# A chunked linear-attention recurrence on 32x32 tiles: delta and state in two halves, each with its own PSUM bank and copy

## The chip, the core and the metric

The kernel runs on one core of a Trainium2 chip. What counts is the device time of one execution in microseconds (us). PE is TensorE (PEld its weight loads), DVE VectorE, ACT ScalarE, POOL GpSimd, SP the SyncE queue that issues the DMAs.

## The reference

One transformer block in Macaron form over 8192 tokens of width 512. Only the middle part is touched: attention of the gated-delta kind with 16 heads of width 32, whose state is carried from token to token.

```python
def _step(Sm, inputs):
    q_t, k_t, v_t, beta_t = inputs
    Sk = jnp.einsum('bhde,bhe->bhd', Sm, k_t)
    delta = v_t - Sk
    Sm = Sm + beta_t[..., None] * jnp.einsum('bhd,bhe->bhde', delta, k_t)
    o_t = jnp.einsum('bhde,bhe->bhd', Sm, q_t)
    return (Sm, o_t)
...
return outputs @ wo + bo
...
x = x + 0.5 * _L0_ffn_ref(_layernorm(x, axis=-1), ...)
x = x + _L0_attn_ref(_layernorm(x, axis=-1), ...)
x = x + 0.5 * _L0_ffn_ref(_layernorm(x, axis=-1), ...)
```

The attention part ends in a feed-forward network of width 2048, for which the kernel splits fp32 factors into two fp32r parts, high and low, and multiplies three times.

## The kernel before, in words

There are three stages. The first (to about 960 us) makes heads, keys and the inner products of the keys and writes them to HBM. The second (about 960 to 1726 us) is the recurrence, and the change lies in it alone. The third (to the end) is the feed-forward network.

The recurrence goes over 256 chunks of 32 tokens. The 16 heads lie as 4 partition groups by 4 column groups, so each product of a chunk is 16 matmuls of 32x32 (function `tiles`); the trace has two passes for each, so 16 matmuls are an x32 of weight loads and of matmuls. A chunk needs six such products, and I call them by their functions: `values` and `keys` (from `ringA`, what DMAs bring), `delta` (`sT` times `nR`, onto `values`), `state` (`de` times `ringB`), and the outputs `out_state` and `out_delta`. Between them ACT copies PSUM to SBUF: `de` after `delta`, `sT` after `state`, `nR` after `keys`. So the chain that carries the state is: delta on PE, copy de, state on PE, copy sT, delta of the next chunk. PE fills the time of a copy with the products of other chunks: `values` and `keys` of a chunk to come, the outputs of a chunk gone by.

PE's program is a real loop (`Fori`) of 64 turns, each one block of 128 tokens, four chunks, and one output product: 12 matmuls of 128x512 with `wo` (`out_product`), for the block before. Since a turn's waits count upward, they wait on registers and stand on an instruction that adds to the register. The other engines' programs are written out, in order of the chunk c, with blk and at from divmod(c, 4). ACT's `high(q)` takes the outputs of a pair of chunks from PSUM as fp32r, DVE's `low(q)` makes the remainder; only when both are there for the pairs of a block may the output product of the block begin (PE waits for `v_olo`). DVE's `add_out` adds the product to `zb`, which ACT made with `normalize` and POOL added a bias to with `add_bo`.

Beside this DVE and POOL solve the triangular systems of chunks 32 and more ahead: `solver(c, 0)` and `solver(c, 1)`, two slots in each chunk with a table of steps that is spread evenly by size. DVE has three of the four column groups (L1474, L1478) and transposes in and out (L1452, L1462), POOL the fourth. In every second block from block 6 to 36 ACT and DVE also split a piece of a weight (DVE's L1517).

SP brings `ringA` and `ringB`, four slots each, in the order of its program; a load of a slot waits until PE is done with it.

## Time and profile before

| | |
|---|---|
| median of 3 runs | 3310.53 us (3310.06 to 3311.02) |
| the profiled execution, its span | 3309.8 us |
| PE busy | 3179.2 us, 96% |
| DVE busy | 1841.6 us, 56% |
| ACT busy | 1308.4 us, 40% |
| POOL busy | 1205.1 us, 36% |
| recurrence, first to last row of its loop | 971.3 to about 1726 us |

The span is the time from the first to the last instruction; here it is within 1 us of the runs' median. PE's busy share says little in the recurrence: a 32x32 matmul takes some 190 ns from start to end but one starts every few ns, so the engine reads as busy through every short wait. What counts there is the time from one start to the next.

### The profile page before, as it was taken

To read this page: it belongs to the slowest core of one execution; us is meant where nothing else is said; L and a number is where in the kernel's file an instruction comes from. 1 tells how busy PE (TensorE), PEld (TensorE's weight loads), DVE (VectorE), ACT (ScalarE), POOL (GpSimd) and SP (SyncE) were. 2 spreads that over 40 slices of the span, in tenths; PEclk is the share of its full clock that TensorE was granted. 3 is DMA by queue.
4 is the path that set the end of the run, shared out by engine and by line. 5 is a ranking of instruction groups with operands and counts; after the bars stand their busy time and mean duration, and the time that the engine had idled before them with its cause. 6 is when DMAs were issued, how large, how long until landed. Compare 5 with 4: busy or idle time off the path is not lost.

```text
span 3309.8 us, 150288 instructions
## 1 busy us (share of the span) xinstructions
PE 3179.2 (96%) x68438; PEld 2594.1 (78%) x68438; DVE 1841.6 (56%) x2965; ACT 1308.4 (40%) x2654; POOL 1205.1 (36%) x1211
## 2 busy tenths in 40 slices
PE   5999999999958999999999999999999999999998
PEld 4777777777747888898888778887777888777886
DVE  6787878778648899888323333233333323333324
ACT  5444445444313333333343333333333433333333
POOL 1435564655526776666211222211222212122211
PEclk8999999999969999999999999999999999999999
DMA  3445555455465677666661110101110110111010
GB/s 111 144 148 167 141 162 154 145 152 162 139 201 181 220 227 228 215 197 207 200 184 35 39 39 13 39 26 39 39 39 17 36 39 26 39 39 38 14 39 26
DMA packets 388865, 356.00 MB, mean 108 GB/s; under 512 B 58256, under 2 KB 321680, under 8 KB 385680
## 3 DMA queue, kind: packets, MB, share of 16 engines
q1 hardware_dynamic: 386400, 351.86, 34.2%
q8 instruction: 154, 2.52, 0.3%
q10 hardware_dynamic: 2224, 0.90, 0.2%
q14 instruction: 87, 0.71, 0.1%
HBM read 184.65 MB, written 153.09 MB: 102 GB/s over the span
## 4 chain that ended last, share of the span: by engine, by line
PE 65%; DMA 2%; SPq 0%; DVE 0%; issue 0%; ACT 0%; DVEq 0%; ACTq 0%
PE bank L237 14%; PE bank L235 14%; PE bank L236 14%; PE bank L1238 13%; PE bank L1283 5%; PE bank L1698 2%; PE bank L1689 2%; DMA ringB<-heads_scratch 1%; PE bank L1681 1%; PE bank L1672 1%; DMA Z<-z_scratch 0%; DVE g L2010 0%; PE bank L1745 0%; SPq L1147 0%; ACT relu L1867 0%
## 5 line engine op out<-in xcount | busy, mean ns | idle before, releaser
L1939 DVE TENSOR_TENSOR glo<-gl,gh 128x512 fp32r<-128x512 f32 x256 | 196.0, 766 | 823.5 <-ACT gh L1817 821.8
L1813 ACT ACTIVATE gl<-bank,b1m 128x512 f32<-128x512 f32 x256 | 176.0, 687 | 736.4 <-PE bank L237 730.9
L235 PE MATMUL bank<-h,w_hi 128*128 128x512 f32 x1024 | 421.1, 411 | 0.1
L235 PE MATMUL bank<-w_hi,gh 128*128 128x512 f32 x1024 | 402.7, 393 | 0.9 <-DVE glo L1939 0.9
L237 PE MATMUL bank<-h,w_lo 128*128 128x512 f32 x1024 | 401.3, 392 | 0.0
L237 PE MATMUL bank<-w_hi,glo 128*128 128x512 f32 x1024 | 400.5, 391 | 0.0
L236 PE MATMUL bank<-h,w_hi 128*128 128x512 f32 x1024 | 399.4, 390 | 0.0
L236 PE MATMUL bank<-w_lo,gh 128*128 128x512 f32 x1024 | 399.2, 390 | 0.0
L236 PEld LDWEIGHTS bank<-h,w_hi 128*128 128x128 f32 x1024 | 193.4, 189 | 49.2 <-issue 10.7
L235 PEld LDWEIGHTS bank<-h,w_hi 128*128 128x128 f32 x1024 | 192.5, 188 | 48.7 <-issue 10.8
L1238 PE MATMUL bank<-ringA 32*32 32x32 f32 x16512 | 221.9, 196 | 5.3 <-issue 4.3
L2076 POOL TENSOR_TENSOR ss<-ss,cst 128x4 f32<-128x4 f32 x15 | 15.3, 1017 | 578.7 <-DVE ss L1922 578.7
L236 PEld LDWEIGHTS bank<-w_lo,gh 128*128 128x128 f32 x1024 | 193.5, 189 | 40.2
L237 PEld LDWEIGHTS bank<-h,w_lo 128*128 128x128 f32 x1024 | 192.3, 188 | 40.8
L235 PEld LDWEIGHTS bank<-w_hi,gh 128*128 128x128 f32 x1024 | 192.5, 188 | 40.1 <-DVE glo L1939 1.3
L237 PEld LDWEIGHTS bank<-w_hi,glo 128*128 128x128 f32 x1024 | 192.3, 188 | 39.8
L967 POOL TENSOR_TENSOR nrm<-nrm,cst 128x16 f32<-128x16 f32 x64 | 185.4, 2897 | 101.3 <-DVE nrm L761 100.6
L1238 PEld LDWEIGHTS bank<-ringA 32*32 32x32 f32 x16512 | 192.1, 105 | 9.8 <-issue 4.6
L1474 DVE TENSOR_TENSOR tmp<-sysf 128x90 f32<-128x90 f32 (+14 forms) x210 | 189.5, 902 | 5.0
L2085 POOL TENSOR_TENSOR Z<-Z,H 128x512 f32<-128x512 f32 x64 | 92.5, 1445 | 273.0 <-DMA H<-x_scratch 273.0
L1478 DVE TENSOR_TENSOR sysf<-sysf,tmp 128x90 f32<-128x90 f32 (+14 forms) x210 | 183.7, 875 | 4.8
L1564 POOL TENSOR_TENSOR zb<-zb,bo 128x512 f32<-128x512 f32 x64 | 93.8, 1465 | 245.7 <-ACT zb L1400 132.0
(200 smaller groups left out, 7086.1 us busy)
## 6 DMA issues: line engine op xcount, KB each, us to landing
ringB<-heads_scratch SPq DMA_DIRECT2D x257, 192.0 KB, 3.3
ringA<-heads_scratch SPq DMA_DIRECT2D x260, 128.0 KB, 2.8
X<-in_L_attn_x SPq DMA_DIRECT2D x16, 1024.0 KB, 10.1
x_scratch<-X SPq DMA_DIRECT2D x16, 1024.0 KB, 4.5
heads_scratch<-vb SPq DMA_DIRECT2D x16, 1024.0 KB, 5.2
heads_scratch<-qk SPq DMA_DIRECT2D x16, 1024.0 KB, 6.6
heads_scratch<-kb SPq DMA_DIRECT2D x16, 1024.0 KB, 5.2
heads_scratch<-kbuf SPq DMA_DIRECT2D x16, 1024.0 KB, 7.2
```

What stands on the lines that cost most here:

```text
L235: e.matmul(o, lhs[0], rhs[0], start=first, stop=False)
L236: e.matmul(o, lhs[0], rhs[1], start=False, stop=False)
L237: return e.matmul(o, lhs[1], rhs[0], start=False, stop=last)
L967: e.tensor_tensor(nrm[:, u], nrm[:, u], pos_half.broadcast_to([P, TC]), ALU.pow).then_inc(o_pow, 1)
L1238: m = e.matmul(out[r, n, :], lhsT[r, n, :], rhs[r, n, :], start=first and n == 0, stop=True, skip_group_check=True)
L1283: m = e.matmul(bank[B_WO][:, :], oh[x][:, f, :], wo[y][:, f, :], start=k == 0, stop=k == 11)
L1474: e.tensor_tensor(tt, N[:, :, j + 1:CH, j:j + 1].broadcast_to([P, 3, rows, j]), N[:, :, j:j + 1, 0:j].broadcast_to([P, 3, rows, j]), ALU.m ...
L1478: e.tensor_tensor(N[:, :, j + 1:CH, 0:j], N[:, :, j + 1:CH, 0:j], tt, ALU.add).then_inc(v_sol, 1)
L1564: e.tensor_tensor(zb[i][:, :], zb[i][:, :], bo[:, :], ALU.add).then_inc(o_yb, 1)
L1813: e.activation(gl[k][:, :], bank[1 - k][:, :], ACT.Gelu_apprx_tanh, bias=b1m[:, m:m + 1]).then_inc(a_gl, 1)
L1939: e.tensor_tensor(gh[k][1][:, :], gl[k][:, :], gh[k][0][:, :], ALU.subtract).then_inc(v_gl, 1)
L2085: e.tensor_tensor(z[:, b, :], z[:, b, :], H[:, b, :], ALU.add).then_inc(o_zx, 1)
```

## The change

`delta` and `state` are each made in two halves of the column groups (0 and 1: FRONT, 2 and 3: BACK), each with its own PSUM bank, its own increment and its own ACT copy of 64 columns in place of one of 128. `values` and `out_delta` are halved with them; `keys` and `out_state` stay whole. The outputs of a chunk are now made within the chunk (before they came one to three chunks later). The output product moves from the end of the loop's turn to its middle, behind chunk 1. PE's waits for ACT and the DMAs are on constants, with one semaphore for each of the four chunks, and PE takes the count back with increments by -2, -16 and -32 on its own matmuls. Only the waits for DVE (`v_olo`, `v_z`) still go by a register. On ACT and DVE the steps of a block stand at other chunks: `high` and `low` at 0 and 2 (before 0 and 1), `normalize` at 1, `add_out` and the piece of a weight at 3, `add_bo` at 2. SP's loads are reordered. The core of the diff:

```diff
-        B_WO, B_R, B_DELTA, B_STATE, B_OUT = 0, (1, 3), (4, 5), 6, (7, 2)
+        B_WO, B_R, B_DELTA, B_STATE, B_OUT = 0, 1, (4, 5), (6, 3), (7, 2)
...
-        a_wohi, a_delta, a_state, a_y2, a_ohi = sems("a_wohi a_delta a_state a_y2 a_ohi")
+        a_wohi, a_y2, a_ohi = sems("a_wohi a_y2 a_ohi")
+        a_delta, a_state = sems("a_delta0 a_delta1 a_delta2 a_delta3"), sems("a_state0 a_state1 a_state2 a_state3")
...
-                if c >= 4 and c % 4 < 2:
-
-                    e.wait_ge(p_delta, max(1, c - 4))
-                elif c >= 4:
-                    e.wait_ge(p_R, c - 3)
+                if c >= 4:
+                    e.wait_ge(p_delta, 2 * (c - 4) + 1)
...
-                    e.wait_ge(p_o, c - 2)
-                e.dma_start(ringB[:, c % 4, :, :], heads_d[c if c < CHUNKS else c - 4, :, Q2:B2 + 1, :]).then_inc(d_B[c % 4], 16)
+                    e.wait_ge(p_o, c - 3)
+                elif c == 3:
+                    e.wait_ge(p_delta, 1)
+                e.dma_start(ringB[:, c % 4, :, :], heads_d[c, :, Q2:B2 + 1, :]).then_inc(d_B[c % 4], 16)
...
             for blk in range(NBLK + 1):
                 c = 4 * blk
-                if c + 6 < CHUNKS + 4:
-                    load_a(c + 6)
-                if blk and c + 3 < CHUNKS:
-                    load_b(c + 3)
-                if c + 7 < CHUNKS + 4:
-                    load_a(c + 7)
                 if c + 4 <= CHUNKS:
+                    load_a(c + 4)
+                if c + 4 < CHUNKS:
                     load_b(c + 4)
+                if blk >= 2:
+                    store_z(blk - 2)
+                if c + 5 < CHUNKS:
+                    load_a(c + 5)
+                    load_b(c + 5)
...
-                if blk >= 2:
-                    store_z(blk - 2)
+                if c + 6 < CHUNKS:
+                    load_a(c + 6)
+                    load_b(c + 6)
                 if 1 <= blk and blk + 1 < NBLK:
                     load_x1(blk + 1)
...
+                if c + 7 < CHUNKS:
+                    load_a(c + 7)
+                    load_b(c + 7)
...
             def tiles(out, lhsT, rhs, first):
 
-                for n in range(GROUPS):
+                made = []
+                for n in range(out.shape[1]):
                     for h in range(4):
                         r = slice(32 * h, 32 * h + 32)
...
+
+            def place(h):
+
+                return split(bank[B_DELTA[h]][:, 0:P // 2])
...
+            def values(j, h):
+
+                return tiles(place(h), split(ringA[:, j, RX, :])[:, own(h), :], split(ringA[:, j, RV, :])[:, own(h), :],
+                             True)
...
+            def delta(j, h):
+
+                made = tiles(place(h), nR[j % 2][:, own(h), :], sT[j][:, own(h), :], False)
+                made[-1].then_inc(p_delta, 1)
+                return made
...
+            def state(j, h):
+
+                tiles(split(bank[B_STATE[h]][:, 0:P // 2]), split(ringB[:, j, RB, :])[:, own(h), :],
+                      de[j % 2][:, own(h), :], False)[-1].then_inc(p_state, 1)
+
+            def out_delta(j, h):
...
+            def chunk(j):
+
+                after, before = (j + 1) % 4, (j + 3) % 4
+                e.wait_ge(a_state[j], 1)
+                made = delta(j, FRONT)
+                made[0].then_inc(d_A[j], -32)
+                made[1].then_inc(a_delta[before], -2)
+                made[2].then_inc(d_B[before], -16)
+                e.wait_ge(d_A[after], 32)
+                keys(after)
+                e.wait_ge(a_state[j], 2)
+                delta(j, BACK)
+                e.wait_ge(d_B[j], 16)
+
+            def outs_back(j):
+
+                made = out_delta(j, BACK)
+                made[0].then_inc(a_state[j], -2)
+                made[-1].then_inc(p_o, 1)
+
+            def rest(j):
+
+                after = (j + 1) % 4
+                out_state(j)
+                e.wait_ge(a_delta[j], 1)
+                state(j, FRONT)
+                values(after, FRONT)
+                out_delta(j, FRONT)
+                e.wait_ge(a_delta[j], 2)
+                state(j, BACK)
+                values(after, BACK)
...
-                ahead(j)
-
-            e.wait_ge(d_A[2], 32)
-            e.wait_ge(d_A[3], 32)
-            e.wait_ge(d_B[0], 16)
+            e.wait_ge(o_s0, 1)
+            for h in (FRONT, BACK):
+                e.matmul(bank[B_STATE[h]][:, 0:P], heads(sT[0][:, :, :]), heads(sT[0][:, :, :]), start=True, stop=True)
+            e.wait_ge(a_delta[3], 2)
             e.wait_ge(d_B[3], 16)
...
-            with e.register("now") as now, e.register("out") as out, e.register("slot_a") as slot_a, \
-                    e.register("next_a") as next_a, e.register("slot_b") as slot_b, e.register("next_b") as next_b:
...
+            keys(0)
+            values(0, FRONT)
+            values(0, BACK)
...
                              hint_back_edge=True, head_slot={mybir.EngineType.PE: 0}):
-                    for j in range(4):
-                        e.wait_ge(a_state, now)
-                        if j == 3:
-                            e.wait_ge(v_olo, out)
-                        e.reg_add(now, now, 1)
...
-                        e.wait_ge(a_delta, now)
...
-                            out_state(3)
-                            out_delta(3)
-                        elif j == 1:
...
-                        else:
-                            e.wait_ge(v_z, out)
-                            e.reg_add(out, out, 4)
-                            out_product(range(12))
-                            e.reg_add(slot_b, slot_b, 16)
...
+
+                    chunk(0)
+                    e.wait_ge(v_olo, out)
+                    e.reg_add(out, out, 4)
+                    rest(0)
+                    outs_back(0)
+
+                    chunk(1)
+                    rest(1)
+                    e.wait_ge(v_olo, out)
+                    e.reg_add(out, out, 4)
+                    e.wait_ge(v_z, done)
+                    e.reg_add(done, done, 8)
+                    outs_back(1)
+                    out_product(range(12))
+
+                    for j in (2, 3):
+                        chunk(j)
+                        rest(j)
+                        outs_back(j)
+
...
             def delta(c):
-                e.wait_ge(p_delta, c + 1)
-                e.activation(heads(de[c % 2][:, :, :]), bank[B_DELTA[(c // 2) % 2]][:, c % 2 * P:(c % 2 + 1) * P],
-                             ACT.Copy).then_inc(a_delta, 2)
+                for h in range(2):
+                    e.wait_ge(p_delta, 2 * c + h + 1)
+                    e.activation(heads(de[c % 2][:, 2 * h:2 * h + 2, :]), bank[B_DELTA[h]][:, 0:P // 2],
+                                 ACT.Copy).then_inc(a_delta[c % 4], 1)
...
-                e.wait_ge(p_o, 2 * q + 3)
+                e.wait_ge(p_o, 2 * q + 2)
...
                     keys(c + 1)
                 state(c)
-                if at < 2 and blk:
-                    high(2 * blk - 2 + at)
+                if at == 0 and blk:
+                    high(2 * blk - 1)
+                elif at == 2:
+                    high(2 * blk)
                 if c == 0:
                     for k in range(NF):
                         split_wo(k)
-                if at == 0 and blk:
+                if at == 1 and blk:
                     normalize(blk - 1)
                 i = piece2(blk)
...
             for c in range(CHUNKS):
                 blk, at = divmod(c, 4)
-                if at == 0 and blk >= 2:
-                    add_out(blk - 2)
+                if at == 3 and blk:
+                    add_out(blk - 1)
                 solver(c, 0)
-                if at < 2 and blk:
-                    low(2 * blk - 2 + at)
+                if at == 0 and blk:
+                    low(2 * blk - 1)
+                elif at == 2:
+                    low(2 * blk)
                 i = piece2(blk)
-                if at == 2 and i is not None:
+                if at == 3 and i is not None:
                     e.wait_ge(a_w1hi, i + 1)
...
-            e.memset(sT[3][:, :, :], 0.0).then_inc(o_s0, 1)
-            e.memset(de[1][:, :, :], 0.0).then_inc(o_s0, 1)
             e.memset(sT[0][:, :, :], 0.0).then_inc(o_s0, 1)
+            e.memset(de[1][:, :, :], 0.0).then_inc(a_delta[3], 2)
+            e.memset(ringB[:, 3, :, :], 0.0).then_inc(d_B[3], 16)
             for c in range(CHUNKS):
                 blk, at = divmod(c, 4)
-                if at == 1 and blk:
+                if at == 2 and blk:
                     add_bo(blk - 1)
```

PE, the part of the loop's turn with the output product, before (`de,ringB` is `state`, L1283 the product):

```order
L1238 MATMUL bank<-ringA 32x32 x16
L1334 REGISTER_ALU [waits d_B3,a_delta]
L1238 MATMUL bank<-de,ringB 32x32 x16
L1349 REGISTER_ALU [waits v_z]
L1283 MATMUL bank<-wo_hi,oT_hi 128x512
L1283 MATMUL bank<-wo_lo,oT_hi 128x512
```

and of the change, behind `state` and `values` of chunk 1 (L1315 is the product):

```order
L1233 MATMUL bank<-de,ringB 32x32 [waits a_delta1]
L1233 MATMUL bank<-de,ringB 32x32 x7
L1233 MATMUL bank<-ringA 32x32 x8
L1346 REGISTER_ALU [waits v_olo]
L1348 REGISTER_ALU [waits v_z]
L1233 MATMUL bank<-ringB,de 32x32 x8
L1315 MATMUL bank<-wo_hi,oT_hi 128x512
```

The wait for DVE's `low` stands right ahead of the product now; before, it stood at chunk 3's `delta`, and the instruction in front of the product waits for `v_z` alone.

DVE, from one `low` to the second next (`oT_lo`), in blocks whose solver steps lie alike, before:

```order
L1491 TENSOR_TENSOR oT_lo<-bank,oT_hi 128x4x64 [waits a_ohi]
L1478 TENSOR_TENSOR sysf<-sysf,tmp 128x3x21x10 [waits v_sol]
L1474 TENSOR_TENSOR tmp<-sysf 128x3x220 [waits v_sol]
L1517 TENSOR_TENSOR w_lo<-Z,w_hi 128x512 [waits a_w1hi]
L1478 TENSOR_TENSOR sysf<-sysf,tmp 128x3x20x11 [waits v_sol]
L1474 TENSOR_TENSOR tmp<-sysf 128x3x228 [waits v_sol]
L1478 TENSOR_TENSOR sysf<-sysf,tmp 128x3x19x12 [waits v_sol]
L1497 TENSOR_TENSOR zb<-bank,zb 128x512 [waits o_yb,p_wo]
L1474 TENSOR_TENSOR tmp<-sysf 128x3x234 [waits v_sol]
L1491 TENSOR_TENSOR oT_lo<-bank,oT_hi 128x4x64 [waits a_ohi]
```

and of the change, from the `low` at chunk 2 to the `low` at chunk 0 of the next block:

```order
L1491 TENSOR_TENSOR oT_lo<-bank,oT_hi 128x4x64 [waits a_ohi]
L1478 TENSOR_TENSOR sysf<-sysf,tmp 128x3x20x11 [waits v_sol]
L1497 TENSOR_TENSOR zb<-bank,zb 128x512 [waits o_yb,p_wo]
L1474 TENSOR_TENSOR tmp<-sysf 128x3x228 [waits v_sol]
L1519 TENSOR_TENSOR w_lo<-Z,w_hi 128x512 [waits a_w1hi]
L1478 TENSOR_TENSOR sysf<-sysf,tmp 128x3x19x12 [waits v_sol]
L1474 TENSOR_TENSOR tmp<-sysf 128x3x234 [waits v_sol]
L1491 TENSOR_TENSOR oT_lo<-bank,oT_hi 128x4x64 [waits a_ohi]
```

Before, the two `low` of a block stand one chunk apart and the rest of the block's work lies behind the second; now they stand two chunks apart, and between the second and the first of the next block lie four solver slots, `add_out` and the piece of a weight.

## Rows read from the trace of the kernel before

**Rows 1.** Stages: busy time by engine (instructions), PEclk, DMA share, GB/s.

```profile
1016.70:1056.00 39.30, 35.66 (x2491) 31.88 (x2478) 38.15 (x43) 13.09 (x48) 37.11 (x35) 0.96 0.71 225
...
1077.60:1592.80 515.20, 509.20 (x35885) 458.97 (x35884) 460.21 (x550) 192.75 (x705) 352.63 (x409) 1.00 0.70 215
1592.80:1609.20 16.40, 13.14 (x781) 11.74 (x780) 8.47 (x7) 4.63 (x17) 1.28 (x1) 0.79 0.76 209
1609.20:1721.00 111.80, 110.75 (x7820) 99.85 (x7822) 17.06 (x35) 42.89 (x158) 13.65 (x11) 1.00 0.67 199
```

**Rows 2.** Timeline, PE, one turn: start, duration, instruction.

```profile
1425.59 0.45 PE L1238 MATMUL bank<-sT,nR 32*32 32x32 f32 x32
...
1429.98 0.45 PE L1238 MATMUL bank<-ringB,sT 32*32 32x32 f32 x30
...
1430.26 0.47 PE L1238 MATMUL bank<-ringB,de 32*32 32x32 f32 x31
1430.70 0.45 PE L1238 MATMUL bank<-ringA 32*32 32x32 f32 x32
1431.03 0.42 PE L1238 MATMUL bank<-de,ringB 32*32 32x32 f32 x29
...
1433.27 0.45 PE L1238 MATMUL bank<-de,ringB 32*32 32x32 f32 x32
1433.65 0.51 PE L1283 MATMUL bank<-wo_hi,oT_hi 128*128 128x512 f32 x1
...
1436.64 0.46 PE L1238 MATMUL bank<-sT,nR 32*32 32x32 f32 x32
```

**Rows 3.** Timeline, the start of a turn on all engines.

```profile
1447.83 0.34 PEld L1238 LDWEIGHTS bank<-sT,nR 32*32 32x32 f32 x32 [0.36 <-issue]
...
1448.11 0.68 DVE L1497 TENSOR_TENSOR zb<-bank,zb 128x512 f32<-128x512 f32 x1
...
1448.71 1.19 DVE L1474 TENSOR_TENSOR tmp<-sysf 128x594 f32<-128x594 f32 x1
...
1449.08 0.20 PE L1238 MATMUL bank<-de,ringB 32*32 32x32 f32 x3
...
1449.41 0.28 ACT L1386 ACTIVATE sT<-bank 128x128 f32<-128x128 f32 x1 [0.54 <-PE bank L1238]
1449.58 0.38 ACT L1393 ACTIVATE oT_hi<-bank 128x256 fp32r<-128x256 f32 x1
...
1450.06 0.42 DVE L1491 TENSOR_TENSOR oT_lo<-bank,oT_hi 128x256 fp32r<-128x256 f32 x1 [0.17 <-ACT oT_hi L1393]
...
1450.40 0.77 DVE L1478 TENSOR_TENSOR sysf<-sysf,tmp 128x594 f32<-128x594 f32 x1
```

**Rows 4.** Groups by line, DVE, 1077.6 to 1592.8 us: busy, mean, idle before.

```profile
L1474 DVE TENSOR_TENSOR tmp<-sysf 128x252 f32<-128x252 f32 (+9 forms) x178 | 161.0, 904 | 4.1
L1478 DVE TENSOR_TENSOR sysf<-sysf,tmp 128x174 f32<-128x174 f32 (+4 forms) x179 | 158.6, 886 | 4.1
L1452 DVE STREAM_TRANSPOSE sysf<-h 128x1024 f32<-128x1024 f32 x20 | 39.0, 1959 | 0.0
L1462 DVE STREAM_TRANSPOSE xt<-sysf 128x1024 f32<-128x1024 f32 x20 | 38.0, 1935 | 0.0
L1491 DVE TENSOR_TENSOR oT_lo<-bank,oT_hi 128x256 fp32r<-128x256 f32 x92 | 37.9, 412 | 14.6 <-ACT oT_hi L1393 14.1
L1497 DVE TENSOR_TENSOR zb<-bank,zb 128x512 f32<-128x512 f32 x46 | 31.7, 688 | 31.9 <-PE bank L1283 19.5 <-issue 12.4
L1517 DVE TENSOR_TENSOR w_lo<-Z,w_hi 128x512 fp32r<-128x512 f32 x15 | 14.1, 937 | 0.0
```

**Rows 5.** Waits, same stretch: total, times, longest.

```profile
PE bank L1238 <- DMA ringB<-heads_scratch: 5.1, 5, 1.3
```

**Rows 6.** Timeline, PE, the first rows of the loop.

```profile
971.32 0.65 PE L1238 MATMUL bank<-sT,nR 32*32 32x32 f32 x32 [6.70 <-issue]
```

**Rows 7.** Timeline, PEld, first stage: 32x32 weight loads.

```profile
302.40 1.88 PEld L408 LDWEIGHTS bank<-qk,rawk 32*32 32x32 f32 x128 [0.35 <-issue]
```

More of the change, by code:

```diff
@@ L1172, in sp_delta @@
             e.dma_start(ln2[:, :], a["L0_attn_ln2_scale"].rearrange("(g p) -> p g", p=P), **SHORT).then_inc(d_bo, 16)
-            for c in range(4, 6):
-                load_a(c)
+            load_b(3)
             load_x1(0)
@@ L1233, in tiles @@
             def tiles(out, lhsT, rhs, first):
-                for n in range(GROUPS):
+                made = []
+                for n in range(out.shape[1]):
                     for h in range(4):
                         r = slice(32 * h, 32 * h + 32)
-                        m = e.matmul(out[r, n, :], lhsT[r, n, :], rhs[r, n, :], start=first and n == 0, stop=True,
-                                     skip_group_check=True)
-                return m
+                        made.append(e.matmul(out[r, n, :], lhsT[r, n, :], rhs[r, n, :], start=first and n == 0,
+                                             stop=True, skip_group_check=True))
@@ L1256, in keys @@
             def keys(j):
-                tiles(split(bank[B_R[j % 2]][:, 0:P]), split(ringA[:, j, RK, :]), split(ringA[:, j, RX, :]),
-                      True).then_inc(p_R, 1)
-            def ahead(j):
-                values(j)
-                keys(j)
-            def delta(j):
-                tiles(place(j), nR[j % 2], sT[j], False).then_inc(p_delta, 1)
-            def out_state(j):
-                tiles(outputs(j), sT[j], split(ringB[:, j, RQ, :]), j % 2 == 0)
-            def state(j):
-                tiles(split(bank[B_STATE][:, 0:P]), split(ringB[:, j, RB, :]), de[j % 2], False).then_inc(p_state, 1)
@@ L1276, in out_delta @@
-            def out_delta(j):
-                tiles(outputs(j), de[j % 2], split(ringB[:, j, RP, :]), False).then_inc(p_o, 1)
+                tiles(split(bank[B_R][:, 0:P]), split(ringA[:, j, RK, :]), split(ringA[:, j, RX, :]),
+                      True)[-1].then_inc(p_R, 1)
+            def delta(j, h):
+                made = tiles(place(h), nR[j % 2][:, own(h), :], sT[j][:, own(h), :], False)
+                made[-1].then_inc(p_delta, 1)
+                return made
+            def out_state(j):
+                tiles(outputs(j), sT[j][:, :, :], split(ringB[:, j, RQ, :]), j % 2 == 0)
@@ new lines, in state @@
+            def state(j, h):
+                tiles(split(bank[B_STATE[h]][:, 0:P // 2]), split(ringB[:, j, RB, :])[:, own(h), :],
+                      de[j % 2][:, own(h), :], False)[-1].then_inc(p_state, 1)
+            def out_delta(j, h):
+                return tiles(outputs(j)[:, own(h), :], de[j % 2][:, own(h), :], split(ringB[:, j, RP, :])[:, own(h), :],
+                             False)
+            def chunk(j):
[10 more added lines that the diff above has]
+                e.wait_ge(d_B[j], 16)
@@ L1287, in pe_delta @@
             e.wait_ge(done1, 5)
-            e.wait_ge(o_s0, 3)
-            e.matmul(bank[B_STATE][:, 0:P], heads(sT[0][:, :, :]), heads(sT[0][:, :, :]), start=True, stop=True)
-            for j in range(2):
-                e.wait_ge(d_A[j], 32)
-                ahead(j)
-            e.wait_ge(d_A[2], 32)
-            e.wait_ge(d_A[3], 32)
-            e.wait_ge(d_B[0], 16)
-            e.wait_ge(d_B[3], 16)
-            with e.register("now") as now, e.register("out") as out, e.register("slot_a") as slot_a, \
-                    e.register("next_a") as next_a, e.register("slot_b") as slot_b, e.register("next_b") as next_b:
-                e.reg_mov(now, 1)
+            e.wait_ge(o_s0, 1)
@@ L1358, in pe_delta @@
-            out_state(3)
-            out_delta(3)
+                    chunk(0)
[10 more added lines that the diff above has]
+                    outs_back(1)
@@ L1435, in act_delta @@
                     e.activation(pieces3[i][1], stage3[i], ACT.Copy).then_inc(a_whi3, 1)
-            high(CHUNKS // 2 - 2)
             high(CHUNKS // 2 - 1)
@@ L1459, in back @@
                     if s >= 2:
-                        for j in range(4):
-                            e.wait_ge(d_A[j], 32 * (NC // 4) * s)
+                        e.wait_ge(p_R, NC * s)
                 e.transpose(xt[(s + 1) % 2][:, :, n, :].rearrange("p c i -> p i c"), sysb[:, n, :, :]).then_inc(v_back, 1)
@@ L1525, in dve_delta @@
                     e.tensor_scalar(H[:, b, :], Z0[:, b, :], ss3[:, b:b + 1], None, ALU.mult).then_inc(v_hs, 1)
-            add_out(NBLK - 2)
-            low(CHUNKS // 2 - 2)
             low(CHUNKS // 2 - 1)
```

79 lines of the change are left out of this document (18 added, 61 removed).

## The prediction

> **What bounds the kernel now.** I read the stages first [rows 1]. Only the recurrence is touched; outside it I expect the same time, and all sums below are over its 64 turns. From 1077.6 to 1592.8 us DVE adds an output product 46 times [rows 4], so a turn takes 515.2 / 46 = 11.20 us. PE reads as busy for 509.2 of the 515.2 us, which says nothing here, and DVE for 460.2, which says much: 10.0 us a turn. In the turns before that (1016.7 to 1056.0) DVE is busy for 38.15 of 39.3 us and is the bound, some 13 us a turn. In the last ten turns (1609.2 to 1721.0, 11.18 us each) the systems are solved and DVE is nearly idle, yet the turn is as long: in the middle PE and its chain set the time, with DVE close behind.
>
> Then one turn of PE, from start to start [rows 2]: 1425.59 to 1436.64 is 11.05 us. A whole product of 16 tiles without a wait takes 0.28 (1429.98 to 1430.26), so 24 of them take 6.7. The output product takes 2.99 (1433.65 to 1436.64). The other 1.34 us are gaps: with a wait between them, the next product starts 0.44 later (1430.26 to 1430.70), 0.33 (1430.70 to 1431.03) or 0.38 (1433.27 to 1433.65), so a wait costs 0.05 to 0.16. A turn has eight waits for ACT, about 0.12 each, 1.0 us.
>
> Last, the rows around a copy [rows 3]. The last tiles of `state` start at 1449.08, ACT's copy at 1449.41: 0.33. The copy takes 0.28 and `high`, which may start 0.17 after it, 0.38. `low` on DVE starts 0.10 behind its end (1449.96 to 1450.06) and lets the next instruction go 0.34 later.
>
> **The change on PE, taken alone.** *Chain.* Before, two whole products (0.56) stand behind `delta` or `state` while its copy is made; the copy is back after 0.33 + 0.28 and the start of PE, some 0.7. Now 40 tiles, 0.70, stand behind each half (`keys`, the other half, `out_state`; or 8 tiles each of `values`, `out_delta`, `state`, `values`, `out_delta`), and the copy is half as wide. From 0.38 for 256 columns and 0.28 for 128 I take 0.23 for 64. So 0.33 + 0.23 + 0.1 = 0.66 fits under 0.70, and the gaps of 1.0 us a turn go. ACT now makes five copies a chunk for three, two more a chunk; it is busy for 192.8 of 515.2 us [rows 1], and eight more of 0.23 a turn leave it at half: hidden. *Added:* 40 groups instead of 24, each a change of operands; not seen apart, between 0 and 0.02 each, I take 0.15 a turn. Three waits stay on registers (`v_olo` twice, `v_z`), the first with the wait for `ringB` ahead of it: 0.25, between 0 and 0.4. The loop's turn stood behind the matmuls of the output product and is now in the open: no row shows it uncovered; the nearest is the 0.36 of issue after the product [rows 3], I take 0.4, bounds 0 and 0.5. The Trainium skill (Advanced Engine Details and Errata, Control Flow Timing) has about 108 ns for a compare-and-branch; by it PE's turn would be 0.3 shorter, which no row here can confirm. The waits on matmuls: in the first stage 128 weight loads of 32x32, with a wait for four semaphores on a matmul in their middle, take 1.88 us without a visible break [rows 7], so I take nothing. PE's own turn: 11.05 - 1.0 + 0.15 + 0.25 + 0.4 = 10.85, between 10.4 and 11.4. Taken alone it would be faster.
>
> **The change on DVE, which decides.** The wait for `low` of a block's second pair moves. That pair's outputs come at the end of a turn, `high` behind chunk 0's copies, `low` after it, and the output product, now in mid-turn, needs `low` one chunk later. The first pair's `high` and `low` come only after chunk 2, behind the product. So there is a ring that no slack breaks: product, chunk 2, `high`, `low`, DVE's work until the next `low`, product. What DVE has to do in it is set by its program: four of a block's eight solver slots, `add_out`, and the piece of a weight. Its length, from the end of the `low` that PE waits for:
>
> - PE starts again 0.10, and its last 8 tiles ahead of the product 0.14: 0.24
> - output product with its edge, 2.99 + 0.10 (0.38 less 0.28) [rows 2]: 3.09
> - chunk 2 up to the end of `state` BACK, 80 tiles, 5 x 0.28: 1.40
> - to the copy 0.33, to `high` 0.17, `high` 0.38, to `low` 0.10, `low` until the next DVE instruction 0.34 [rows 3]: 1.32
> - four solver slots: (161.0 + 158.6 + 39.0 + 38.0) / 46 = 8.62 us a block, with the idle 8.2 / 46 = 0.18 [rows 4], 8.80; half: 4.40
> - `add_out`, 1448.11 to 1448.71 [rows 3]: 0.60
> - the piece of a weight, 0.94 in 15 of 46 turns [rows 4]: 0.31
> - the second `low`: 0.42
>
> Sum 11.78 us, and 12.4 in a turn with a piece of a weight, against 10.85 of PE alone. The slots aren't even (a transpose is 1.95 us, others under 0.5): turns with little work fall back on PE's own and save less than the full ones lose. I add 0.15: 11.93. The other four slots lie beside the first part of the ring, 0.24 + 3.09 + 1.40 + 0.98 = 5.7 us against 4.4: DVE idles there for what it lacks later.
>
> **The sum**, against the execution's 3309.8 us:
>
> - 46 turns at 11.93 for 11.20: +34. The 5.1 us that PE waited for `ringB` [rows 5] are inside the 11.20, and loads now have three chunks
> - the first turns: DVE has the same work and no gap either way: 0
> - the turn from 1592.8 to 1609.2, 16.4 us [rows 1], late behind a 1 MB load and at a granted clock of 0.79: its loads are asked for earlier, -3 (0 to -5)
> - the last ten turns, 10.85 for 11.18: -3 (-8 to +2)
> - the start: PE sat 6.7 us before the loop [rows 6], since it waited for the slot of chunk 3; that slot is now filled with zeros on chip: -4 (0 to -5)
>
> 3309.8 + 24 = 3334 us, and against the median of 3310.5, less than 1 us from it, the same 3334.
>
> SP's loads cost nothing: `ringA` of a chunk is asked for at the start of the chunk four earlier, `ringB` at its end, so both have over 5 us, and the queue's order follows these waits. If that cover goes, a late load costs about 1 us, as the five did [rows 5].
>
> **Rivals.**
> *DVE is not late.* If `low` is always there in time, all turns but the first are PE's own: 46 x (10.85 - 11.20) = -16, and -10 for the rest: 3284 us, 3258 with PE at 10.4. For it speaks that DVE idles for 1.1 us a turn today [rows 4]; against it that this idle time is spread over the turn today, and that the ring's terms are all measured. It decides if the ring is under 11.1, 0.7 below my sum.
> *The two cancel.* DVE is late only in turns with a piece of a weight: 15 turns at 12.2, 31 at 10.9, so +15 and -9, and -10 for the rest: 3306 us.
> *PE itself is slower.* The 24 waits for ACT and the DMAs that now stand on matmuls, and PE's own takings-back, could cost like the gaps of today. At 0.12 each PE's turn is 13.7 and the time 3310 + 62 x 2.5 = 3465; it decides from 0.05 each, where PE's turn reaches 12.0. Against it stand rows 7. The Trainium skill (TensorE: Matmul & The Clock Gate, The cost: per-tile semaphore tail) gives each increment of a matmul 26.3 ns at the tail; the change has ten a chunk for four, so by that rule up to 0.6 a turn, PE's at 11.5. That is still inside the ring and would add 6 us in the last ten turns: 3340. No run shows it yet.
>
> **How the numbers follow.** The ring as summed: 0.70, from 3317 to 3358 (the slots' work 5% either way is 0.2 a turn, 10 us; the unevenness as much; start and end 8). DVE not late: 0.14. Cancelling: 0.10. PE slower, over 3360: 0.06. The range reaches from 3304 to 3360 and leaves out the fast case and the slowest. What a measurement can tell from no change is 0.2%, 7 us: faster 0.15, same 0.12, slower 0.73.
>
> **What the changed profile would show.** If right: in the middle turns PE waits for DVE's `oT_lo` ahead of the second half of chunk 1's `out_delta`, 0.5 to 1.5 us a turn; turns near 11.1 and near 12.5 alternate up to block 36; DVE waits for ACT's `oT_hi` at chunk 2; the last ten turns are under 11.2; the gaps around ACT's copies are gone. Wrong, if PE doesn't wait for `oT_lo`, or if its turn without DVE is above 11.5. It would also be wrong if DVE's operations grow or shrink with what POOL does beside them, since POOL's `add_bo` moves by a chunk.

## The result and the profile after

The changed kernel takes 3334.31 us (median of 4 runs, 3333.07 to 3337.02) beside 3310.78 us for the kernel before (4 runs): a ratio of 1.0071, with a 95% interval from 1.0058 to 1.0083. It is slower by 0.7%; 3334 was forecast. Its profiled execution has a span of 3331.8 us, 22.0 more than the 3309.8 of before.

The same view by stretches as in [rows 1], of the changed kernel. The borders are the starts of the same turns, taken from the first tile behind the output product (which ends a turn in the kernel before and stands in its middle now):

```profile
1028.00:1067.90 39.90, 35.82 (x2368) 31.88 (x2368) 39.14 (x44) 17.01 (x70) 26.75 (x30) 1.00 0.71 231
1067.90:1611.10 543.20, 511.16 (x35885) 463.99 (x35888) 450.14 (x548) 260.84 (x1073) 333.42 (x405) 1.00 0.66 204
1611.10:1636.90 25.80, 23.04 (x1561) 20.89 (x1560) 13.24 (x19) 12.11 (x50) 5.44 (x10) 0.93 0.76 214
1636.90:1727.80 90.90, 88.32 (x6245) 80.59 (x6246) 13.22 (x29) 46.77 (x191) 11.36 (x9) 1.00 0.67 205
```

The second row holds the same 46 turns as the second of [rows 1]: 543.2 us for 515.2, that is 11.81 a turn for 11.20, +28 us. The third row is two turns, one of them behind the 1 MB load: 25.8 us for the same two turns' 27.5 before. The last is 8 turns: 90.9 us, 11.36 each; the kernel before has 89.4 for the same eight. At the start the loop begins at 968.9 us and no longer at 971.3, and the first tile behind product 6 comes 9.7 us earlier; 3.3 of these come back at the end, since two chunks now follow the last product. So -6.4 + 28 - 1.7 + 1.5 is 21.4, and the span is 22.0 longer.

Chain of the page: the share of each engine in the work that ended last.

```profile
PE 62%; DVE 5%; issue 2%; DMA 1%; ACT 1%; SPq 0%; DVEq 0%; ACTq 0%
```

The waits from 1067.9 to 1611.1 us (who waits, for whom: total, times, longest):

```profile
DVE oT_lo L1491 <- ACT oT_hi L1393: 84.9, 46, 4.8
PEld bank L1233 <- issue: 51.8, 118, 1.0
...
PE bank L1233 <- ACT sT L1385: 14.7, 46, 0.4
PE bank L1233 <- DVE oT_lo L1491: 14.3, 22, 0.9
PEld bank L1233 <- DMA ringA<-xt: 2.9, 3, 2.0
```

PE waits 22 times for DVE's `oT_lo`, 14.3 us in all. In [rows 4] DVE waited 14.1 us for ACT's `oT_hi`; now it waits 84.9, once a turn, at chunk 2. The work of DVE is nearly what it was, 450.1 us busy for 460.2 in these 46 turns: `add_out` 46 times and 675 ns, the solver's products 918 ns and additions 832 ns for 904 and 886.

The ring as the timeline of DVE shows it, 1141.65 to 1154.15 us, start and duration:

```profile
1141.65 0.42 DVE L1491 TENSOR_TENSOR oT_lo<-bank,oT_hi 128x256 fp32r<-128x256 f32 x1 [1.68 <-ACT oT_hi L1393]
1141.99 0.48 DVE L1478 TENSOR_TENSOR sysf<-sysf,tmp 128x324 f32<-128x324 f32 x1
...
1142.85 0.68 DVE L1497 TENSOR_TENSOR zb<-bank,zb 128x512 f32<-128x512 f32 x1
...
1144.15 0.68 DVE L1519 TENSOR_TENSOR w_lo<-Z,w_hi 128x512 fp32r<-128x512 f32 x1
...
1145.70 1.95 DVE L1462 STREAM_TRANSPOSE xt<-sysf 128x1024 f32<-128x1024 f32 x1
1147.50 0.40 DVE L1491 TENSOR_TENSOR oT_lo<-bank,oT_hi 128x256 fp32r<-128x256 f32 x1
1147.82 3.83 DVE L1462 STREAM_TRANSPOSE xt<-sysf 128x1024 f32<-128x1024 f32 x2
1153.81 0.42 DVE L1491 TENSOR_TENSOR oT_lo<-bank,oT_hi 128x256 fp32r<-128x256 f32 x1 [2.17 <-ACT oT_hi L1393]
1154.15 1.92 DVE L1462 STREAM_TRANSPOSE xt<-sysf 128x1024 f32<-128x1024 f32 x1
```

And PE beside it, timeline: the two late starts, and the first tiles behind four output products.

```profile
1127.75 0.33 PE L1233 MATMUL bank<-sT,nR 32*32 32x32 f32 x16
...
1139.15 0.33 PE L1233 MATMUL bank<-sT,nR 32*32 32x32 f32 x16
...
1148.12 0.33 PE L1233 MATMUL bank<-ringB,de 32*32 32x32 f32 x16 [0.74 <-DVE oT_lo L1491]
...
1151.32 0.33 PE L1233 MATMUL bank<-sT,nR 32*32 32x32 f32 x16
...
1162.69 0.33 PE L1233 MATMUL bank<-sT,nR 32*32 32x32 f32 x16
```

From one first-pair `low` to the next is 12.16 us (1141.65 to 1153.81): DVE works without a break up to the second `low` (1147.82), PE starts 0.30 later, makes its product and chunk 2, and the next first `low` is through at 1154.15, 6.33 us after the second one. The turns are 11.40, 12.17 and 11.37 long. The late one is the one with a piece of a weight in it, and up to block 36 these pieces come in every second block: of the 16 such turns twelve take 12.07 to 12.37 us, and four 11.86. Of those without a piece only four are as late, 12.23 to 12.39, every eighth. No transpose lies in their ring, but the solver's largest steps do: in the first of them the `low` start at 1082.48 and 1088.38, 5.90 us apart, with steps of 504 to 594 elements between them. The others are PE's own or within 0.1 of it, near 11.4 (but for one of 11.95 and one of 11.67), and so are nearly all from block 38 on (11.35 to 11.7, one of 13.25).

### The profile page after: what moved, and what is told of

It is laid out like the page before. It is cut to its first block, busy times and chain, and to the rows that moved or that the text cites. A ratio compares the mean times of both kernels' runs of the same rounds, so it can differ in the third digit from the quotient of the medians.

```text
span 3331.8 us, 149311 instructions
## 1 busy us (share of the span) xinstructions
PE 3178.0 (95%) x68312; PEld 2596.9 (78%) x68312; DVE 1831.2 (55%) x2965; ACT 1403.4 (42%) x3166; POOL 1186.3 (36%) x1211
## 4 chain that ended last, share of the span: by engine, by line
PE 62%; DVE 5%; issue 2%; DMA 1%; ACT 1%; SPq 0%; DVEq 0%; ACTq 0%
PE bank L237 14%; PE bank L235 14%; PE bank L236 14%; PE bank L1233 10%; PE bank L1315 6%; PE bank L1698 2%; PE bank L1689 2%; DVE sysf L1478 1%; DVE tmp L1474 1%; PE bank L1681 1%; PE bank L1672 1%; DMA ringA<-xt 1%; DVE oT_lo L1491 1%; DVE zb L1497 0%; DVE w_lo L1519 0%
## 5 line engine op out<-in xcount | busy, mean ns | idle before, releaser
L1233 PE MATMUL bank<-ringA 32*32 32x32 f32 x16448 | 331.9, 195 | 11.8 <-issue 6.7
L1233 PEld LDWEIGHTS bank<-ringA 32*32 32x32 f32 x16448 | 261.7, 105 | 8.6 <-DMA ringA<-xt 4.5
L1379 ACT ACTIVATE de<-bank 128x64 f32<-128x64 f32 x512 | 114.2, 223 | 324.6 <-PE bank L1233 317.9
L1233 PE MATMUL bank<-sT,nR 32*32 32x32 f32 x8192 | 176.8, 197 | 27.8 <-ACT sT L1385 19.8
L1233 PE MATMUL bank<-ringB,de 32*32 32x32 f32 x8192 | 176.8, 194 | 24.3 <-DVE oT_lo L1491 20.7
```

What stands on the lines that cost most here:

```text
L1233: made.append(e.matmul(out[r, n, :], lhsT[r, n, :], rhs[r, n, :], start=first and n == 0, stop=True, skip_group_check=True))
L1379: e.activation(heads(de[c % 2][:, 2 * h:2 * h + 2, :]), bank[B_DELTA[h]][:, 0:P // 2], ACT.Copy).then_inc(a_delta[c % 4], 1)
```

## The experiments

All twelve stand against the kernel before on the same chip, where it took medians of 3312 to 3313 us; so ratios are compared, and 0.001 is 3.3 us. "A turn" is the mean of 40 turns, from the first tile behind product 12 to the one behind product 52; by it the kernel before takes 11.19 us and the changed one 11.80.

### The ring on DVE: e1_low_first, e2_early_add, e3_both

```diff
-                solver(c, 0)
                 if at == 0 and blk:
                     low(2 * blk - 1)
-                elif at == 2:
+                solver(c, 0)
+                if at == 2:
                     low(2 * blk)
```

> Edit: at chunk 0 of a block DVE makes low of the block before ahead of its solver slot, not behind it; one slot of about 1.1 us leaves the ring product, chunk 2, high, low, slots, low, product. Theory (the DVE ring is what makes the middle turns long): the ring falls from 11.8 to about 10.7 us, under PE's own turn of 11.37 as the last ten turns of the changed kernel show it; 45 middle turns take 11.80 us on average, so up to 45 x 0.43 = 19 us go: 3334 - 15 to -19 = 3315 to 3319 us, PE's waits for oT_lo nearly gone, the last ten turns unchanged. Rival (PE's own work is longer and the waits for oT_lo only replace others): under 3 us, 3331 to 3335.

Measured: ratio 1.0037 (1.0023 to 1.0051), 11 us less than the changed kernel. The median turn is 11.41, PE's own, and PE waits for `oT_lo` no more. But the mean is 11.67: five turns, every eighth, take 14.71, 13.56, 14.67, 13.27 and 14.94 us, and the last four of them lie in the 40. The waits of the stretch 1080 to 1600 us show what is late there; behind them the row of the first of these turns on PE's timeline:

```profile
PEld bank L1233 <- DMA ringA<-xt: 9.7, 5, 2.2
PE bank L1233 <- DMA ringA<-xt: 9.2, 5, 2.0
```

```profile
1130.93 0.45 PE L1233 MATMUL bank<-ringA 32*32 32x32 f32 x32 [1.64 <-DMA ringA<-xt]
```

So the ring was what made the alternate turns long, and once it is short another wait comes up, every eighth turn.

```diff
-                if at == 3 and blk:
+                if at == 2 and blk:
                     add_out(blk - 1)
...
-                elif at == 2:
-                    low(2 * blk)
...
-                if at == 3 and i is not None:
+                if at == 2 and i is not None:
...
+                if at == 2:
+                    low(2 * blk)
                 solver(c, 1)
```

> Edit: add_out and the low piece of a weight move from DVE's chunk 3 to its chunk 2, ahead of low of the first pair, where DVE idles for ACT's oT_hi; solver slots stay. Theory (DVE ring): 0.6 us leave the ring in every turn and 0.94 more in the 15 turns with a piece; those turns go from about 12.2 to 11.4, the others to 11.37: -12 to -19 us, 3315 to 3322. Rival (PE's own work): under 3 us. Against both: if the piece now makes the first low late by more than DVE idled there, the gain is under 8 us.

Measured: 1.0061 (1.0047 to 1.0074), only 3 us less; its interval overlaps that of the changed kernel. PE's waits for `oT_lo` fall from 13.6 us to 1.2 in the stretch from 1080 to 1600 us, and its median turn is 11.42, so the ring is gone here too, and DVE's wait for `oT_hi` falls from 81.4 to 30.7 us; the same five turns, up to 14.9, take the gain back.

> Both edits at once. Theory: the ring is under 10.2 us and no turn of the middle waits for DVE's oT_lo; what is left is PE's own turn of 11.37: no more than 3 us better than the better of the two alone, 3313 to 3318 us, so still not faster than the kernel before (3311), since PE's own turn is 0.3 longer than the 11.05 of before. Rival (ring still decides after one edit): the gains of the two add up, to 3300 to 3308.

Measured: 1.0049 (1.0035 to 1.0062): no better than the first edit alone. The gains don't add up: PE's own turn and the long turns are what is left (14.94, 13.07, 11.76, 15.64 and 13.22 us at the same places). The forecast time (3313 to 3318) was too low by those turns.

### The 2 MB load: e5_split_load, e10_before_split

The five turns lie at the blocks at which SP issues the load of a system's input, `lt`: 2048 KB, 8.7 us from issue to landing, ahead of the loads of the next two chunks in the queue. In e5 it goes in four pieces, in four blocks:

```diff
-                if c % NC == 12 and c // NC + 2 < NS:
-                    load_system(c // NC + 2)
+                if c % NC in (4, 8, 12, 16) and c // NC + 2 < NS:
+                    load_system(c // NC + 2, c % NC // 4 - 1)
```

> Edit: low first, and the 2 MB load of a system's input, which SP issues in one piece at the block whose first chunk is 12 of 32, goes in four pieces of 0.5 MB at the blocks of chunks 4, 8, 12 and 16. Theory (with the DVE ring short, what is left over PE's own turn are the turns in which PE's operands queue behind that load): in the profile of low first the five such turns take 71.2 us for 5 x 11.39, 14.2 us too many; in pieces of a quarter they take under 0.5 us too many each: -10 to -14 us, 3311 to 3315 us. Rival (these turns are long since DVE or ACT is late there, and the DMA only came last): under 3 us, 3322 to 3327.

Measured: 1.0008 (0.9999 to 1.0017), 10 us less than e1_low_first. All of the 40 turns are now between 11.30 and 11.48, mean 11.41. With these two corrections the changed kernel can't be told from the one before, and what it is short of now is PE's own turn.

> The kernel before with one edit, the 2 MB load of a system's input in four pieces. Theory (the load holds up the operands behind it in the queue): before, PE waited for ringB five times, 5.1 us, in turns of 12.0 to 12.4 for 11.05: -4 to -6 us, ratio 0.9983 to 0.9988. Rival: those turns are long for DVE's work: no change.

Measured: 0.9987 (0.9978 to 0.9996), 3306.95 us. The turns of 12.0 to 12.4 at the same blocks become 11.1, and the mean turn falls from 11.19 to 11.09. In the old order the same load cost about 1 us a time, in the new one 2 to 3.5 (e1_low_first). Why the full changed kernel shows only one such turn (13.25) isn't settled: its late turns give the loads time, but no run took that apart.

### PE's own turn: e4_both_rotated, e6_split_rotated, e7_groups_cut, e8_more_waits, e9_spare_signals, e11_register_waits

PE's own turn was forecast at 10.85 us and is 11.36 to 11.41. Five runs take its terms apart. The first cuts the loop elsewhere:

```diff
-                with nc.Fori(0, NBLK, 1, engines=bass.OrderedEngineSet([mybir.EngineType.PE]),
...
+                first()
+                with nc.Fori(0, NBLK - 1, 1, engines=bass.OrderedEngineSet([mybir.EngineType.PE]),
...
+                    second()
+                    first()
+                second()
```

Here `first` stands for chunks 0 and 1 with the output product, `second` for chunks 2 and 3.

> Both edits, and PE's loop cut at another place: chunks 0 and 1 with the output product stand once ahead of the loop, its body is chunk 2, chunk 3, chunk 0, chunk 1, product, so that the loop's turn lies behind the product's twelve matmuls as it did before. Theory (the uncovered turn of the loop costs PE 0.4 to 0.5 us a turn): turns fall from 11.37 to 10.9, 56 turns by 0.45 = -25 us against the kernel with both edits, so about 3290, faster than both kernels; the extra code ahead of the loop costs up to 8 us once, when its instructions are fetched. Rival (the gap at the loop's turn is the wait for ACT's state copy, and not the turn itself): no change, 3313 to 3318.

Measured: 1.0025 (1.0013 to 1.0036), 8 us less than e3_both, where 17 to 25 were expected. The turn did fall, from a median of 11.41 to 10.99. But the profile shows the price at both ends: from the first tile behind product 0 to that behind product 6 it takes 87.0 us for 80.1, and the last two chunks, outside the loop, end some 5 us later than inside it. The long turns at the 2 MB load are in it too, up to 15.07.

> Low first, the load in four pieces, and the loop cut so that its turn lies behind the output product. Theory (the three corrections are independent): the turn is 10.97 us as in the profile of the rotated kernel, 0.42 less than 11.39, 56 turns: -23 us, and the code that is fetched outside the loop gives back 13: -10 us against the kernel with the load in pieces, 3301 to 3305, faster than before. Rival (at 10.97 the DVE ring, 10.7 with uneven slots, is late again): a gain under 4 us, 3308 to 3314, with PE's waits for oT_lo back.

Measured: 0.9982 (0.9973 to 0.9991), 9 us less than e5_split_load. The mean turn is 11.04, 0.37 less. The rival is right in a small part: PE waits for `oT_lo` again. All its waits for another engine or a transfer from 1080 to 1600 us are these:

```profile
PE bank L1235 <- DMA ringA<-xt: 1.9, 1, 1.9
...
PE bank L1235 <- ACT de L1388: 1.3, 1, 1.3
PE bank L1235 <- DVE oT_lo L1500: 1.0, 4, 0.3
```

The row that is missing tells most. In the changed kernel PE waited 46 times for ACT's `sT`, 0.32 us each, always at chunk 0. ACT's copies are the same here, and the wait is gone: it was the turn of the loop, and the copy was only the last release that the trace had seen before it. The trace of the changed kernel has the branch itself, PE's L1334 (the three figures are the least, median and largest duration in ns). Behind the one of 1142.97 us the first weight load comes at 1143.41, with 0.40 us of idle time ahead of it that no wait explains:

```profile
L1334 PEldq COMPARE_BRANCH  x65: 80/216/3380, 965.3 to 1742.8; - x65
1143.41 0.21 PEld L1233 LDWEIGHTS bank<-sT,nR 32*32 32x32 f32 x13 [0.40 <-issue]
```

> Against e5_split_load: values and out_delta of a half are made in turns of 4 tiles (4 + 4 + 4 + 4) and not 8 and 8, except the second half of chunk 1. The same 384 tiles a turn, 14 more changes between groups of operands. Theory (a change of operands and bank costs 0.03 us, which is why the 40 groups of the changed kernel cost 0.5 us and not the 0.15 of the forecast): +0.42 us in 60 turns, +25 us (15 to 30) over e5_split_load. Rival (changes cost nothing and the longer turn comes from the waits that sit on matmuls): under 3 us.

Measured: 1.0012 (1.0003 to 1.0021), a turn of 11.40 for 11.41. Fourteen more changes of operands a turn cost nothing. This theory falls.

> Against e5_split_load: every fourth 32x32 matmul waits for a semaphore with a constant that was reached long ago, 96 such waits a turn where there were some 28. Theory (a satisfied constant wait on a matmul costs nothing): under 3 us. Rival of the forecast (PE itself slower by its waits): at 0.005 us each +29 us, at 0.03 each +170 us.

Measured: 1.0076 (1.0062 to 1.0090), a turn of 11.84: 0.43 us for 96 waits, 4.5 ns each. This is a mean of two kinds: the trace has 23 more semaphore instructions a turn, so some 73 of the 96 stand on matmuls and the rest as instructions of their own. Not nothing, but the 24 that the change puts on matmuls are 0.11 us a turn; the rival's 0.12 us each is out.

The signals:

```diff
-                tiles(outputs(j), sT[j][:, :, :], split(ringB[:, j, RQ, :]), j % 2 == 0)
+                made = tiles(outputs(j), sT[j][:, :, :], split(ringB[:, j, RQ, :]), j % 2 == 0)
+                for k in range(4, 12):
+                    made[k].then_inc(p_spare, 1 if k % 2 == 0 else -1)
```

> Against e5_split_load: eight matmuls in the middle of out_state of every chunk signal a semaphore that nobody waits for (+1, -1 in turn), 32 more signals a turn where there are 40. Theory (signals are what lengthens PE's own turn: the changed kernel has ten a chunk for four, and in its trace the second half of keys, behind the three takings-back, takes 0.24 us for 0.145 in every chunk): the second half of out_state grows likewise; by the 0.38 us for 24 signals 0.5 us a turn, +30 us; the Trainium skill's page TensorE: Matmul & The Clock Gate (The cost: per-tile semaphore tail) gives 26.3 ns for each increment, which would be 0.84 us a turn, +50 us. Rival (signals cost nothing, the stall in keys comes from elsewhere, as the wait for ringA at its head): under 4 us.

Measured: 1.0134 (1.0119 to 1.0150), 3356.65 us, 42 us above e5_split_load and between the two sizes expected; a turn of 12.10: 0.69 us for 32 signals, 22 ns each. The timeline shows the place. First e5_split_load, the tiles behind `out_state`; then the same in e9_spare_signals:

```profile
1299.96 0.31 PE L1235 MATMUL bank<-de,ringB 32*32 32x32 f32 x13
...
1300.13 0.28 PE L1235 MATMUL bank<-ringA 32*32 32x32 f32 x12
...
1300.26 0.29 PE L1235 MATMUL bank<-ringB,de 32*32 32x32 f32 x13
...
1300.39 0.31 PE L1235 MATMUL bank<-de,ringB 32*32 32x32 f32 x13
```

```profile
1328.83 0.38 PE L1235 MATMUL bank<-de,ringB 32*32 32x32 f32 x14
...
1329.08 0.39 PE L1235 MATMUL bank<-ringA 32*32 32x32 f32 x13
...
1329.32 0.33 PE L1235 MATMUL bank<-ringB,de 32*32 32x32 f32 x13
...
1329.49 0.31 PE L1235 MATMUL bank<-de,ringB 32*32 32x32 f32 x13
```

Without signals the three steps from start to start are 0.17, 0.13 and 0.13 us; with them 0.25, 0.24 and 0.17. The place was misjudged: the delay doesn't show at the tiles that signal, in the middle of `out_state`, but at the two groups behind. Over 38 turns these two take 0.24 and 0.25 us for 0.15 and 0.13, so 0.21 for eight signals, 26 ns each; 22 is what is left of it in the turn, since chunks 1 and 3 grow by 0.20 us, but chunks 2 and 0, which had small gaps, by 0.17 and 0.15. In the same way the three takings-back at `delta` FRONT show in the second half of `keys`.

> Against e5_split_load: four more waits of PE against a register, each with a register addition behind it, on a value reached long ago, two in chunk 2 and two in chunk 3. Theory (three such waits cost the changed kernel about 0.3 us a turn where 0.25 was taken): 0.1 each, 0.4 a turn, +25 us (20 to 30). Rival (what stands in the trace there is the wait for ringB and for the copies, which would be waited for anyway): under 5 us.

Measured: 1.0031 (1.0018 to 1.0043), a turn of 11.53: 0.12 us for four, 0.03 each. It lies between theory and rival: a third of what was expected. The gaps of 0.16 and 0.15 us that e5_split_load has at its own register waits are then mostly something else, and no run took that apart.

How long the turn is can be read off two rows of PE's timeline, 40 turns apart. Of e5_split_load, e8_more_waits, e9_spare_signals and e12_all_split in this order:

```profile
1137.11 0.33 PE L1235 MATMUL bank<-sT,nR 32*32 32x32 f32 x16
...
1593.54 0.33 PE L1235 MATMUL bank<-sT,nR 32*32 32x32 f32 x16
```

```profile
1137.96 0.33 PE L1236 MATMUL bank<-sT,nR 32*32 32x32 f32 x16
...
1611.58 0.33 PE L1236 MATMUL bank<-sT,nR 32*32 32x32 f32 x16
```

```profile
1141.45 0.33 PE L1235 MATMUL bank<-sT,nR 32*32 32x32 f32 x16
...
1625.60 0.33 PE L1235 MATMUL bank<-sT,nR 32*32 32x32 f32 x16
```

```profile
1135.72 0.33 PE L1238 MATMUL bank<-sT,nR 32*32 32x32 f32 x16
...
1577.35 0.33 PE L1238 MATMUL bank<-sT,nR 32*32 32x32 f32 x16
```

### The best version: e12_all_split

```diff
-                    e.dma_start(Z0[:, :, :], z_v[0]).then_inc(d_x[0], 16)
+                if READY2 <= blk < READY2 + NB:
+                    b = blk - READY2
+                    e.dma_start(Z0[:, b, :], z_v[0][:, b, :]).then_inc(d_zp if b < NB - 1 else d_x[0], 16)
```

> Against e6_split_rotated: the 1 MB load of Z0 at block 52 in four pieces as well, one a block. Theory (the one long turn near block 54, 15.6 us there, is late behind that load): that turn falls to 11 to 13: -2 to -4 us, ratio to before 0.997 to 0.9976. Rival (the turn is long for another load or for the pieces of the next stage's weights): no change from 0.9982.

Measured: 0.9971 (0.9961 to 0.9981), 3303.02 us: 0.3% faster than the kernel before. The turn behind the load, 15.57 us in e6_split_rotated, is 11.01. The turn is 11.04 on average. The chain of its page has DVE at 2% and PE at 67%, where the changed kernel has 5% and 62%:

```profile
PE 67%; DVE 2%; issue 1%; DMA 0%; ACT 0%; SPq 0%; DVEq 0%; ACTq 0%
```

How much of this is the change itself isn't shown. With `lt` in four pieces on both sides it is 0.9982 (e6_split_rotated) beside 0.9987 for the kernel before (e10_before_split), and the intervals overlap. The split of `Z0` gives 0.11% more here, but no run gives it to the kernel before, whose turn at that load is still 15.30 us in e10_before_split, some 4 us over its neighbours. By that estimate it would come to about 3303 us as well. So the loads are what the 0.3% can be put down to, and the halves may be worth nothing: their turn of 11.04 stands beside 11.09.

## Why the prediction was right, and where its sizes were off

**The mechanism.** The forecast was a ring over DVE that no slack breaks, and it stood. PE's waits for it are 0.3 us a turn (14.3 in 46), less than the 0.5 to 1.5 forecast. As summed it is 11.47 without a piece of a weight and 12.4 with one; the ring of 1141.65 to 1153.81 has one and takes 12.16. The part outside DVE is 6.33 us for the 6.05 of the sum, and the piece takes 0.60 from its start to the next one's (1144.15 to 1144.75), not the 0.94 of its duration. DVE waits for `oT_hi` at chunk 2 in every turn, as said. Taking one slot out of the ring (e1_low_first), or `add_out` and the piece (e2_early_add), ends PE's waits for `oT_lo`, but for 1.2 us in e2_early_add. Of the signs that were named, the alternation held (11.4 and 12.2 for 11.1 and 12.5), and the last turns failed: under 11.2 was forecast and 11.36 measured.

**The 46 turns: +28 us for the +34 forecast.** The mean turn is 11.81 for 11.93, but put together otherwise. I had every turn as long as the ring. In fact the ring is longer than PE's own turn only where a piece or the solver's largest steps lie in it, in some twenty turns, much as the rival *the two cancel* had it (it named the 15 with a piece); and the others fall back on PE's own turn, which is not 10.9 but 11.4. Two errors, one on each side, leave the sum 6 us too high. Of the 0.61 us a turn (11.80 for 11.19 in the 40 turns), e1_low_first and e5_split_load together take 0.39 away and 0.22 remain. PE's own turn is more than that: the 11.19 holds the kernel before's own waits behind the 2 MB load, and beside e10_before_split (11.09) it is 0.32 longer, 15 us in 46 turns.

**PE's own turn: 11.36 for the 10.85 forecast** (11.4 was its upper bound). This is the step that failed in size, by its terms:

- *signals*: taken at nothing in the sum and left to a rival. The change has ten signals a chunk for four, 24 more a turn; at 22 ns each (e9_spare_signals) that is 0.52 us, an estimate, since signals were added and no run took the change's own away. The Trainium skill (TensorE: Matmul & The Clock Gate, The cost: per-tile semaphore tail) gives 26.3 ns for each at the tail of a group of tiles; measured are 26 at the place and 22 in the turn, and by that rule the prediction's rival had PE at 11.5. The run with spare signals bears the rule out; [rows 7] couldn't speak against it, as they tell of waits.
- *waits on matmuls*: taken at nothing, 4.5 ns each (e8_more_waits), 0.11 a turn. [rows 7], with waits at one place among 128 weight loads, were too coarse for that.
- *changes of operands*: 0.15 taken, nothing measured (e7_groups_cut).
- *the loop's turn*: 0.4 taken, 0.37 to 0.42 measured (e6_split_rotated, e4_both_rotated). The Trainium skill (Advanced Engine Details and Errata, Control Flow Timing) has about 108 ns for a compare-and-branch; the trace doesn't agree. Its 65 records of this loop have a median of 216 ns, in the kernel before too, where the product covered it, and the whole turn of the loop costs over three times the page's figure when it is uncovered. The prediction said that no row could confirm the shorter turn; these records of its own trace spoke against it.
- *register waits*: 0.25 taken for three; 0.03 each for satisfied ones (e11_register_waits), the gaps around the real three are larger.
- *the gaps at the copies*: 1.0 taken away. The trace has no such gap left once the turn of the loop is covered (e6_split_rotated); no run put the whole copies back, so the 1.0 itself is read and not tested.

With these: 11.05 - 1.0 + 0.52 + 0.11 + 0.4 + 0.1 (registers) is 11.18, and about 0.2 stay open. The first candidate are the gaps around the three real register waits: in e5_split_load `delta` BACK of chunk 0 takes 0.31 us for 0.15 and `values` BACK of chunk 1 0.28 for 0.13, of which the sum has 0.1. No run took these waits away.

**The last turns.** Forecast 3 us gained in ten; the last eight take 90.9 us for 89.4: 1.5 lost. The same error, PE's own turn.

**The start and the turn behind the 1 MB load.** -4 and -3 forecast, about -6 and -2 measured. But the loop begins only 2.4 us earlier; the other 4 come from the first turns, which were put at nothing, and no run took them apart.

**The total.** Against a span of 3331.8 us the sum was 3333.8. The turns were put 6 us too high, the last ones 4 to 5 too low, the start 2 too high and the turn behind the load 1 too low: that 3334 came out to the microsecond is luck, and what the forecast earned is the way and the rough size.

**SP's loads cost nothing: wrong, but hidden.** I looked at each chunk's loads, and not at the 2 MB one that now goes ahead of two chunks' loads that have less lead. It shows as 2.5 us of waits in the changed kernel and as 14 us as soon as DVE's ring is short (e1_low_first: five turns of 71.2 us for 5 x 11.39). That is why correcting the ring gave 11 us and not the 15 to 19 expected.

**The rivals.** *DVE is not late* needed 3284 us. That is out: with DVE not late (e5_split_load) it is 3316. *The two cancel* was nearly right on which turns are late, and out by the 0.5 us of PE's own turn: with 11.4 and not 10.9 it doesn't cancel. *PE itself is slower* by 0.12 a wait is out (e8_more_waits), but by its signals it is slower, 0.5 us a turn by the estimate above, and this rival had a part in the result.

## What to carry to other kernels

Splitting work into halves to hide a copy pays with signals and waits: count them, and price them (here 22 ns for a signal, 4.5 for a wait on a matmul) against the gap that they close. Where a result is handed round over several engines once a turn, sum the ring, and look what an engine does in program order between two of its steps; moving one independent instruction out of it is cheap. When the longest wait has gone, look for the large load in the queue ahead of the small ones, and cut it into pieces.

## What the runs showed of the hardware that was not expected

- A signal on a 32x32 matmul in a stream without gaps costs 22 ns (e9_spare_signals, 32 more a turn: +0.69 us; half of them counted down, and the two signs were not separated), and its delay shows some 12 to 20 tiles later, not where the signal is.
- Each added, satisfied wait for a constant in such a stream costs 4.5 ns (96 a turn: +0.43 us, 23 of them as instructions of their own); a satisfied wait against a register with an addition behind it 30 ns (four a turn: +0.12 us).
- A change of operands and output bank between groups of tiles costs nothing that can be measured, even every four tiles (11.40 for 11.41 us a turn).
- The uncovered turn of PE's loop costs 0.37 to 0.42 us; its compare-and-branch has a median of 216 ns. Cutting the loop elsewhere saves this, but gives back some 5 us at the start and as much at the end, once (e4_both_rotated beside e3_both: 6.9 us more up to product 6, less 2.2 that the first product comes earlier).
- A load of 2 MB took 8.7 us from issue to landing and held up the small loads behind it by up to 4.2 us of PE's time (a turn of 15.64 for 11.41 in e3_both).
